# Six steps of three V products instead of seven uneven ones, and the denominators' transposes two steps sooner, in a fused attention block

## The reference

```
q = (x @ Wq + bq);  k = (y @ Wk + bk);  v = (y @ Wv + bv)      # y: 8192 context tokens
attn = softmax(q k^T / sqrt(32));  out = attn @ v               # per head
```

## Time and profile before

| | us |
|---|---|
| median of 3 runs | 2995.61 (2994.95 to 2996.25) |
| the profiled execution | 2997.04 |
| its span | 2995.2 |
| PE busy | 2904.2 (97%) |
| DVE busy | 2205.6 (74%) |
| ACT busy | 1671.3 (56%) |
| POOL busy | 2044.9 (68%) |

### The profile page before, as it was taken

One profiled execution on the slowest core, in us unless ns is written; L12 is line 12 of the kernel. 1 busy time (PEld: TensorE's weight loads), 2 busy tenths in 40 slices (PEclk: granted clock), 3 DMA queues, 4 the chain that ended last, 5 costly groups with the idle time before them and its releaser, 6 DMA issues.

```text
span 2995.2 us, 41476 instructions
## 1 busy us (share of the span) xinstructions
PE 2904.2 (97%) x14776; PEld 1827.8 (61%) x14776; DVE 2205.6 (74%) x3296; ACT 1671.3 (56%) x2956; POOL 2044.9 (68%) x761
## 2 busy tenths in 40 slices
PE   7999999999999999999999999999999887899999
PEld 4666666666666666666666666666544333445587
DVE  7777777777777777777777777777646999987653
ACT  1467676666667666666666666666631565422021
POOL 1599999999999999999999999999930000002000
PEclk9999999999999999999999999999989998999999
DMA  5544454444435455443544444444250112215100
GB/s 163 133 99 109 98 117 101 97 110 103 114 90 119 101 121 139 111 110 86 117 101 108 100 109 111 92 113 102 69 184 27 41 47 99 85 56 170 70 15 18
DMA packets 145760, 296.26 MB, mean 99 GB/s; under 512 B 36050, under 2 KB 41170, under 8 KB 135986
## 3 DMA queue, kind: packets, MB, share of 16 engines
q1 hardware_dynamic: 135908, 226.76, 27.6%
q0 software_dynamic: 9072, 66.06, 11.8%
q10 hardware_dynamic: 576, 0.79, 0.1%
HBM read 114.47 MB, written 8.06 MB: 41 GB/s over the span
## 4 chain that ended last, share of the span: by engine, by line
PE 90%; DVE 6%; ACT 1%; SPq 1%; issue 1%; POOL 0%; DMA 0%; DVEq 0%; POOLq 0%; ACTq 0%
PE ps L1905 17%; PE ps L1931 16%; PE ps L1944 15%; PE ps L1857 9%; PE ps L1881 9%; PE ps L1888 9%; PE ps L2161 4%; PE ps L2125 3%; PE ps L2141 3%; PE ps L1961 2%; PE ps L1913 1%; DVE bx L1344 1%; SPq L671 1%; DVE pm L1082 1%; PE ps L2153 1%
## 5 line engine op out<-in xcount | busy, mean ns | idle before, releaser
L1082 DVE TENSOR_REDUCE pm<-ps 128x1 f32<-128x512 f32 x2048 | 1403.3, 691 | 539.3 <-PE ps L1905 457.6
L1579 ACT ACTIVATE pf<-ps 128x512 f32<-128x512 f32 x2048 | 1203.5, 603 | 655.0 <-PE ps L1931 572.0
L925 POOL TENSOR_TENSOR psum<-psum,pf 128x2048 f32<-128x2048 f32 x317 | 1456.0, 4593 | 18.7
L1905 PE MATMUL ps<-ks,qs 96*128 96x512 f32 x2048 | 833.4, 407 | 10.3 <-DMA qs<-QL 3.6
L1931 PE MATMUL ps<-qs,ks 98*128 98x512 f32 x2048 | 814.8, 399 | 1.6 <-ACT pf L1579 1.6
L1905 PEld LDWEIGHTS ps<-ks,qs 96*128 96x128 f32 x2048 | 386.9, 189 | 197.9 <-issue 109.5
L1944 PE MATMUL ps<-pf,V 128*32 128x512 f32 x4096 | 472.5, 602 | 0.0
L1931 PEld LDWEIGHTS ps<-qs,ks 98*128 98x128 f32 x2048 | 391.4, 191 | 46.3 <-ACT pf L1579 12.5
L940 POOL TENSOR_TENSOR ring_r<-ring,w_hi 128x512 fp32r<-128x512 f32 x16 | 21.8, 1374 | 550.8 <-ACT w_hi L1812 550.8
L925 POOL TENSOR_TENSOR psum<-pf 128x2048 f32<-128x2048 f32 x64 | 308.9, 4827 | 51.2 <-ACT pf L1579 51.2
L1881 PE MATMUL ps<-cTh,Wkg 128*128 128x512 f32 x732 | 301.0, 411 | 0.2 <-POOL cTl L889 0.2
(11 more groups left out here) (237 smaller groups left out, 3045.3 us busy)
## 6 DMA issues: line engine op xcount, KB each, us to landing
ks<-KH SPq DMA_DIRECT2D x1024, 64.0 KB, 2.0
psum<-pf POOLq DMA_DIRECT2D x63, 1024.0 KB, 8.8
ks<-KL SPq DMA_DIRECT2D x512, 64.0 KB, 2.0
cT<-in_ctxT SPq DMA_DIRECT2D x32, 768.0 KB, 6.9
Wkg<-wk_rows SPq DMA_DIRECT2D x61, 384.0 KB, 3.1
BC<-bc_rows SPq DMA_DIRECT2D x32, 512.0 KB, 4.8
ring<-in_ffn_w SPq DMA_DIRECT2D x16, 1024.0 KB, 8.0
wA<-in_W_fcT SPq DMA_DIRECT2D x4, 1024.0 KB, 11.5
```

What stands on the lines that cost most here:

```text
L925: pool.tensor_tensor(acc, before, pf[:, tile % P_SLOTS, :], ALU.add).then_inc(s_sum, 1)
L1082: dve.tensor_reduce(pm[:, of % 2, n // BLK, n % BLK:n % BLK + 1], src, AX.X, ALU.max).then_inc(s_wfree, 1)
L1579: act.activation(pf[:, tile % P_SLOTS, j * NTOK:(j + 1) * NTOK], ps[:, S_BANK + u % S_BANKS, :], ACT.Exp, scale=SCALE).then_inc(s_exp, 1)
L1905: last = pe.matmul(dst, qs[0:3 * HD, h, t * P:(t + 1) * P], ks[0:3 * HD, keys_of(of, j), i * 512:(i + 1) * 512], start=True, stop=True)
```

## The change

The V units are laid on six steps of three products each, steps 17 to 22 and 1 to 6. Steps 23, 24 and 7, 8 then have no side pieces. K units stay as they were. D comes two steps sooner, at step 22 in place of 24; the loop is two steps shorter for it.

```diff
-D_LAG = 9
+D_LAG = 7
...
 PIECES = {"K": TERMS, "V": VM * TERMS}
-PIECES_AT = {kind: [range(r * n // SIDE_STEPS, (r + 1) * n // SIDE_STEPS) for r in range(SIDE_STEPS)]
+STEPS_OF = {"K": SIDE_STEPS, "V": SIDE_STEPS - 1}
+PIECES_AT = {kind: [range(r * n // STEPS_OF[kind], (r + 1) * n // STEPS_OF[kind]) for r in range(STEPS_OF[kind])]
              for kind, n in PIECES.items()}
...
     n, r = divmod(i + SB_AHEAD + SIDE_EARLY, SIDE_SPAN)
     g, n = divmod(n, len(SIDE_UNITS))
-    if g + SIDE_AHEAD < NGT and r < SIDE_STEPS:
+    if g + SIDE_AHEAD < NGT and r < STEPS_OF[SIDE_UNITS[n][0]]:
         return (SIDE_UNITS[n][0], g + SIDE_AHEAD, SIDE_UNITS[n][1]), PIECES_AT[SIDE_UNITS[n][0]][r]
```

## The result

The changed kernel takes 3022.42 us (median of 4 runs, 3021.07 to 3026.57) against 2995.93: a ratio of 1.0094, 95% interval 1.0082 to 1.0107. It is slower by 0.9%, about 26.5 us; 29 were forecast. The profiled execution took 3026.57 (span 3024.8), the slowest of the four, and is 29.5 us above the profiled one of before.

The account below looks back on a forecast made before the run. PE, busy 97% of the span, was taken as the bound. Empty-step waits less K's saved wait 23.2, D -0.3, cast 6.6, first group -0.2: 29.3 us on 2995.61 gave 3025 us, range 3012 to 3033.

Parts of the forecast that it names:

- The wait at the two empty steps: Two empty steps behind a V unit: PE wants 0.94 us, the work banks allow 1.28, a new 0.34 us wait.
- line 1905's waits for line 1082: Sign that the forecast is right: A's loads wait for DVE's maximum some 120 times more.
- DVE's idle time doesn't help: Two empty steps: DVE idling in loaded steps doesn't remove the 0.34 us wait, one item's latency through two banks.
- K's wait of 0.125 us goes: K's first product behind a V unit: its 0.125 us wait for ACT's copy goes, 108 times.
- Steps of three: Six loaded V steps: no cost in themselves; bound 0.82 to 0.84 us a step, 7 us either way.
- The cast's wait: Step 28 in 14 groups: S waits behind ACT's cast, 0.47 us lost each time, 6.6 us in all.
- The sum: Whole kernel: 23.2 - 0.3 + 6.6 - 0.2 = 29.3 us slower, 3025 us.
- The clock: Rival: PE's brief stops twice a group halve the clock; 207 us over 61 groups, 3232; chance 0.01.
- Only the copy's wait counts: Rival at the empty steps: bank wait hidden, 108 x 0.125 = 13.5 us gained, 2982; chance 0.04.
- taken back later: Rival: a burst waits anyway, so most of the loss vanishes there; between 2990 and 3001; chance 0.03.
- the bank wait without the cast's: Rival: S at step 28 isn't held up behind the cast; 22.7 us, 3018; chance 0.14.
- a wait of 0.25 and not 0.34: Two empty steps: bank free before the maximum's profiled end, next maximum 0.60 behind, not 0.69; 9.7 us less, 3015.

Follow-up runs that it names:

- V ahead of S: Kernel before, with a V unit's last-step products between A and S and ACT's copy ahead of that step's exponential: 2992.71 us, ratio 0.9997.
- the half maximum: Changed kernel with the row maximum at steps 7 and 23 over 256 of 512 columns: 2997.72 us; same at steps 4 and 20: 3023.09.
- Both edits together: Kernel before with V ahead of S and K units laid as 2, 1, 1, 1, 1, 1, 2 products: 2984.74 us, ratio 0.9968.
- V ahead with D and the cast moved: Kernel before with V ahead of S, D at step 22 and the context's first cast at step 32: 2994.87 us, ratio 1.0001.
- the spread casts: Both edits together, plus D at step 22 and the first half's three casts at steps 24, 27 and 30, one each: 2994.76 us, ratio 1.0005.
- POOL's second part sooner: Both edits together, plus POOL's part of the context's second half one add sooner: 2983.96 us, ratio 0.9970.

## Why the prediction was right, and where it wasn't

**The wait at the two empty steps.** Right in place and size: 1.28 or 1.29 us for 0.94, loads idle 0.51 "by DVE", 122 such waits. With K's 0.125 saved, steps 7 to 9 lose 0.22 us a unit in the mean of the trace, and 0.215 was forecast. Shown by putting the empty steps apart (29 us back), and by halving the one maximum that counts against halving another. One of the signs that I gave was badly put: line 1905's waits for line 1082 don't grow by 120 in number (116 before, 125 after), since most of the loads waited before too, hidden.

**DVE's idle time doesn't help.** Right: leaving out DVE work at steps 4 and 20 changes nothing.

**K's wait of 0.125 us goes.** Right for this change, since the S of step 10 stands where it is due, 0.235 behind its A. As a gain that could be had by itself it was wrong: before, 0.10 of it lay over a bank wait that I hadn't seen, because I worked out the 1.28 for the empty step with the step ahead of it (1.30) and not with the one behind it (1.175). The kernel with V ahead of S showed that, with the row of 0.51 and the 10.0 us at steps 10 and 26.

**Steps of three.** Here the sum was short: it put this at nothing and kept it for the range. I took 0.83 and gave 0.84 as the bound; they run at 0.84 (980.62 to 981.46). The six loaded steps, 976.33 to 981.46, are 5.13 us here, not 5.06; the mean over the V1 units of the trace is 5.11, so 0.05, or 6 us over 123 units. The period of 32 steps shows the same: it grows by 0.51 in groups without D, where 0.43 was forecast. With an empty step in their middle the same steps go at 0.82 to 0.84 in the mean, six in a row go at 0.84 from the fourth on. Why is open.

```profile
976.33 0.50 PE L1906 MATMUL ps<-ks,qs 96*128 96x512 f32 x1
```

**The cast's wait.** Right in kind, too big: the load of step 28's S comes 0.47 behind its A, where 0.235 is due, and 0.10 more, so 0.34 us are lost and not 0.47. Missed, in the working for the groups with D, was that D at step 22 makes that step 1.27 long and lets ACT catch up: its exponential of step 23 comes 0.68 behind the A of that step (931.83, 932.51), not 0.80. The first group, which has no D, bears that out: there the 0.47 came (its load idle 0.65, step 28 0.49 longer than without the wait). In the kernel with D's move alone D is at step 22 too and the loss is the full 0.66, so it takes the two empty steps as well. The first group's load of step 28's S, and then the timeline of a group with D, A of step 23, ACT from the copy on, A and S of step 28:

```profile
130.83 0.19 PEld L1932 LDWEIGHTS ps<-qs,ks 98*128 98x128 f32 x1 [0.65 <-ACT pf L1580]
```

```profile
931.83 0.41 PE L1906 MATMUL ps<-ks,qs 96*128 96x512 f32 x1
932.03 0.59 ACT L1566 COPY V<-ps 128x512 f32<-128x512 f32 x1 [0.20 <-PE ps L1889]
932.51 1.09 ACT L1580 ACTIVATE pf<-ps 128x512 f32<-128x512 f32 x2
933.48 1.67 ACT L1537 CAST cTh<-cT 128x512 fp32r<-128x512 f32 x3
935.03 2.08 ACT L1580 ACTIVATE pf<-ps 128x512 f32<-128x512 f32 x4
...
935.23 0.39 PE L1906 MATMUL ps<-ks,qs 96*128 96x512 f32 x1
935.70 0.50 PE L1932 MATMUL ps<-qs,ks 98*128 98x512 f32 x1
```

**The sum.** 29.3 forecast; 30.7 in the attention of the profiled executions; 26.5 between the medians. Added up by step over the two traces, steps 1 to 10 and 17 to 25 are 27.8 us longer, step 28 is 4.4 longer, and all the others together 1.5 shorter. Against the forecast the steps of three are the plus (6 us), the cast (14 x 0.13 = 1.8) the minus. Executions of the changed kernel differ by 5.5 us (3021.07 to 3026.57), so that the number came within 3 us is in part luck: two errors of the terms work against each other, and the last 3 us can't be told apart.

**The rivals.** The clock: its mean over the span is 0.984 in the changed kernel and 0.983 in the one before, and through the attention (105 to 2187 us) the granted clock is 1.00, the 2.4 GHz level; nothing. "Only the copy's wait counts" was refuted by the waits of 0.51; "taken back later" by the 26.5 us; "the bank wait without the cast's" by the 14 waits at step 28. The case of a wait of 0.25 and not 0.34 (3015) would have the A of step 9 0.09 sooner; it is 1.18 behind that of step 7, and the load waits for the end of the maximum.

**Wrong among the expectations of the experiments** were the half maximum (2985 for 2997.72), mostly for the 0.10 of a late load that it left out, and V ahead of S (2982 for 2992.71), for the bank wait under the copy's. Both edits together (2979 to 2982 for 2984.74) fell short by POOL's part. Of those that moved the cast, the changed kernel with it at step 32 (3017 for 3022.01) is not settled by the time, V ahead with D and the cast moved (2976 for 2994.87) failed for the bank wait and for POOL, and the spread casts (2974 to 2976 for 2994.76) for POOL, which I had taken for idle enough; POOL's second part sooner (2979 to 2980 for 2983.96) moved the wait elsewhere. The six steps with an empty one between (2996 to 3002 for 2991.49) were a little faster than expected.

## What to carry to other kernels

With n buffers between two engines the limit isn't on the mean step but on every n steps in a row (shown here for n = 2): any two successive steps must last 1.28 us (0.43 until the reader starts, 0.69 of reading, 0.06 to the load, 0.10 for a load that isn't hidden), so short steps belong between long ones. Check a new arrangement against that sum at every neighbour, the one behind as well. Where a wait is to be taken away, look for a second one that ends just before it: here taking away either alone brought nothing that could be told, and only both together did (2992.71, 2994.71, and 2984.74 together).

## What the runs showed that was not expected

A maximum over 512 columns takes 690 ns in the mean and one over 256 columns 424: 266 ns for 256 columns and, if the time grows evenly with the columns (two sizes were measured), 158 that don't depend on the size. The two groups of the kernel with half maxima at steps 7 and 23 (xcount | busy us, mean ns | idle before):

```profile
L1084 DVE TENSOR_REDUCE pm<-ps 128x1 f32<-128x512 f32 x1920 | 1312.1, 690 | 558.2 <-PE ps L1907 461.3
...
L1084 DVE TENSOR_REDUCE pm<-ps 128x1 f32<-128x256 f32 x128 | 54.3, 424 | 20.7 <-PE ps L1907 4.9
```

A small transposing job can be useful by its mere length: D's 0.43 us kept PE from running into the three casts on ACT, and moving it two steps away lost 5.7 us net.

The stop of 1.60 us in the kernel with the cast at step 32 had a sequel: the granted clock is 1.00 up to it and 0.50 (the 1.2 GHz level) from about 1082.9 to 1086.2, so that steps 12 and 13 of that group take 1.71 and 1.28 us where they take 0.94 and 0.70 elsewhere. The 15 stops of 1.1 to 1.5 us in the kernel with the spread casts, and the two of 0.34 us per group in the changed kernel, left it at 1.00.
